# Setup of a two-layer attention and feed-forward kernel: where the first steps' moves, loads and mask work are issued

## The reference

```
x = x + cross_attention_0(layernorm(x), ctx, mask, Wq, bq, Wk, bk, Wv, bv, Wo, bo)   # 16 heads of 16, 77 context tokens
x = x + experts(layernorm(x))             # 6 experts of width 128, top 2 by a router
x = x + cross_attention_1(layernorm(x), ctx, w_q, w_kv, w_concat)                    # 16 query heads, one shared key/value head
x = x + fixed_point_mlp(layernorm(x))     # 256 -> 1024 -> 256, piecewise linear gelu, rounding to 1/256
# attention: softmax(q k^T / 4 + mask) v, for 77 keys a batch
```

## Time and profile before

| what | value |
|---|---|
| median of 3 runs | 789.33 us (789.02 to 789.87) |
| the profiled execution's own time | 787.69 us |
| its span | 785.5 us |
| TensorE busy | 729.2 us, 93% |
| VectorE, ScalarE, GpSimd busy | 644.6, 514.0, 373.0 us |

### The profile page before, as it was taken

The page is one execution under the profiler, slowest core; times in us unless marked ns, Lnnn a source line. Parts: engine busy times, 40 slices in busy tenths (PEclk is TensorE's granted clock), DMA queues, the critical chain, the costliest instruction groups (busy, mean ns, idle before and its releaser), DMA issues.

```text
span 785.5 us, 13554 instructions
## 1 busy us (share of the span) xinstructions
PE 729.2 (93%) x4372; PEld 549.3 (70%) x4372; DVE 644.6 (82%) x1546; ACT 514.0 (65%) x943; POOL 373.0 (47%) x323
## 2 busy tenths in 40 slices
PE   4799999999999999999997999999989999999995
PEld 3566666766558888888874555555568888888985
DVE  7648778777878878888897888998788999999995
ACT  3446556565654456555436777677778989989885
POOL 6374444334222223232214232232259999999884
PEclk9889999999999999999999999999999999999999
DMA  7975634654210000001029665755200000000001
GB/s 234 134 209 121 139 76 93 119 120 88 68 36 1 1 1 7 1 1 55 1 41 143 89 82 76 131 76 77 30 1 1 2 28 28 28 28 2 28 28 54
DMA packets 25101, 48.64 MB, mean 62 GB/s; under 512 B 3686, under 2 KB 7016, under 8 KB 24520
## 3 DMA queue, kind: packets, MB, share of 16 engines
q1 hardware_dynamic: 23366, 46.54, 30.6%
q10 hardware_dynamic: 1666, 1.24, 0.5%
HBM read 12.12 MB, written 4.19 MB: 21 GB/s over the span
## 4 chain that ended last, share of the span: by engine, by line
PE 54%; DVE 19%; issue 8%; ACT 7%; DMA 7%; POOL 4%; SPq 0%; ACTq 0%; DVEq 0%; POOLq 0%
PE bank L141 15%; PE bank L649 6%; PE bank L436 6%; PE bank L413 6%; DMA qst<-mt 5%; PE bank L424 5%; PE bank L388 5%; DVE mx L342 4%; PE bank L416 3%; DVE fpart L768 3%; PE bank L812 3%; PE bank L391 2%; DVE x L617 2%; DVE fyl L780 2%; DVE ffixed L762 2%
## 5 line engine op out<-in xcount | busy, mean ns | idle before, releaser
L316 ACT ACTIVATE pt<-bank 77x512 f32<-77x512 f32 x256 | 141.1, 589 | 78.2 <-PE bank L416 58.3
L342 DVE TENSOR_REDUCE mx<-bank 128x4 f32<-128x308 f32 x256 | 109.0, 471 | 22.5 <-PE bank L391 12.3
L413 PE MATMUL bank<-qst,l_kst 128*77 128x512 f32 (+1 forms) x256 | 102.8, 417 | 15.8 <-DMA qst<-mt 9.8
L721 POOL TENSOR_TENSOR frise<-fg,fg 128x512 f32<-128x512 f32 x64 | 101.3, 1583 | 6.7 <-ACT fg L739 1.5
L388 PE MATMUL bank<-l_kblk,qh 128*128 128x308 f32 x256 | 81.3, 336 | 10.1 <-DVE mx L342 5.7
L284 POOL TENSOR_TENSOR ol<-ot,oh 128x512 fp32r<-128x512 f32 x32 | 41.4, 1294 | 94.4 <-ACT oh L321 50.2
L617 DVE SCALAR_TENSOR_TENSOR x<-bank,eweight,x 128x256 f32<-128x256 f32 x192 | 79.6, 477 | 4.1 <-PE bank L649 3.8
L413 PEld LDWEIGHTS bank<-qst,l_kst 128*77 128x77 f32 (+1 forms) x256 | 36.5, 146 | 65.1 <-ACT pt L316 24.1
L103 POOL TENSOR_TENSOR rstd<-var,minus_half 128x4 f32<-128x4 f32 x32 | 34.4, 1076 | 100.1 <-DVE var L98 52.2
L114 ACT ACTIVATE xn<-x,shift,rstd 128x256 f32<-128x256 f32 (+1 forms) x128 | 67.2, 594 | 17.1 <-POOL shift L105 17.1
L388 PEld LDWEIGHTS bank<-l_kblk,qh 128*128 128x128 f32 x256 | 48.0, 192 | 42.8 <-issue 33.1
(11 more groups left out here) (176 smaller groups left out, 2117.0 us busy)
## 6 DMA issues: line engine op xcount, KB each, us to landing
qst<-qh SPq DMA_DIRECT2D x64, 256.0 KB, 6.5
qst<-ql SPq DMA_DIRECT2D x32, 256.0 KB, 8.8
out<-x SPq DMA_DIRECT2D x8, 512.0 KB, 2.6
qst<-ml SPq DMA_DIRECT2D x8, 480.0 KB
x<-in_x SPq DMA_DIRECT2D x3, 1024.0 KB, 12.4
weights<-in_mlp_w SPq DMA_DIRECT2D x2, 1024.0 KB, 5.0
mraw<-in_mask SPq DMA_DIRECT2D x8, 154.0 KB
x<-in_x SPq DMA_DIRECT2D x2, 512.0 KB, 5.8
```

Source lines behind the costliest of these rows:

```text
L316: self.nc.scalar.activation(self.pt[0:T, i // 4 % 2, i % 4, :], self.bank_of(G, i)[0:T, :], ACT.Exp).then_inc(self.probs, 1)
L342: self.nc.vector.reduce_max(out, banks[u % len(banks)][:, 0:4 * T].rearrange("q (p par t) -> q p par t", p=2, par=2), AX.X).then_inc(self. ...
L413: last = self.nc.tensor.matmul(out, layer.kst[rows, layer.stack(c * HC + 2 * k + par), b * T:(b + 1) * T], self.qst[rows, self.slot(G), c ...
L721: self.nc.gpsimd.tensor_tensor(self.rise[:, k % 2, :], self.g1[:, k % self.R, :], self.g0[:, k % self.R, :], ALU.subtract).then_inc(self.r ...
```

## The change

Seven edits, all in the setup and in steps 0 to 2. (1) The move of block 0's maxima is issued by ScalarE instead of SyncE. (2) The values of batch 0 are computed between the turn of block 0 and its query projection; batches 1 to 3 stay behind the maxima, and ScalarE takes the first two batches' values before the norm of block 1. (3) The two loads of the last 2 MB of `x` leave the setup; each stands in step 0 and step 1 of SyncE's program, behind that step's query moves and ahead of the next mask's load and of `stack_maxima`, with a semaphore of its own. (4) The load of mask 1 is issued between the two halves of step 0's moves. (5) GpSimd builds the key blocks of batches 1 to 3 as soon as VectorE has written those of batch 0, ahead of the inversion for block 1. (6) GpSimd splits mask 1 before step 0's loop and not in it. (7) In step 0 the projection of block 1's queries stands behind scores 1 and 2 instead of 0 and 1, ScalarE's `leading` behind exponentials 2 and 4 instead of 0 and 1, VectorE's second `rest` behind maxima 0 and 1, and units 2 and 3 stand at i = 6 instead of 4.

```diff
--- before.py
+++ after.py
@@ -873,7 +873,7 @@
         fw1 = raw(0, F)
         fw2 = weights[:].rearrange("p (c d) -> p c d", d=D)
 
-        x0_in, x1_in, x2_in, xr_in = sem("x0_in"), sem("x1_in"), sem("x2_in"), sem("xr_in")
+        x0_in, x1_in, x2_in, xr_in = sem("x0_in"), sem("x1_in"), sem("x2_in"), [sem(f"xr_in{k}") for k in range(2)]
         k_in, q_in, c_in, vo_in = sem("k_in"), sem("q_in"), sem("c_in"), sem("vo_in")
         cleared = sem("cleared")
         kst_clear, kst_const = sem("kst_clear"), sem("kst_const")
@@ -911,21 +911,18 @@
                         for k, part in enumerate((l0.kh, l0.kl, l0.kh)):
                             sp.dma_start(l0.kst[32 * k + 16 * par:32 * k + 16 * par + 16, c * HC + par:(c + 1) * HC:2, :].bitcast(F32),
                                          part[64 * par:64 * par + 64, c, :].bitcast(F32)).then_inc(kst_in[c], 16)
+                    att.stack_queries(sp, 0, c)
                     if c == 0:
-                        att.stack_queries(sp, 0, 0)
-                att.stack_maxima(sp, 0)
-                att.stack_queries(sp, 0, 1)
-                att.load_mask(sp, 1, d["mask"])
-                for b in range(2, B):
-                    tiles = slice(2 * b * NT, 2 * (b + 1) * NT)
-                    sp.dma_start(x[:, tiles, :], d["x"][:, tiles, :]).then_inc(xr_in, 16)
-
+                        att.load_mask(sp, 1, d["mask"])
                 for G in range(BLOCKS):
                     n = G + 1
                     if n < BLOCKS:
                         att.stack_low(sp, n)
                         for c in range(C):
                             att.stack_queries(sp, n, c)
+                        if G < 2:
+                            tiles = slice(2 * (G + 2) * NT, 2 * (G + 3) * NT)
+                            sp.dma_start(x[:, tiles, :], d["x"][:, tiles, :]).then_inc(xr_in[G], 16)
                         if n + 1 < BLOCKS:
                             att.load_mask(sp, n + 1, d["mask"])
                         att.stack_maxima(sp, n)
@@ -997,20 +994,21 @@
                 att.mask_parts(pool, 0)
                 nc.gpsimd.memset(att.pt[64:P, :, :, :], 0.0).then_inc(pt_clear, 1)
                 pool.wait_ge(pt_clear, 1)
-                norm.invert(pool, 1)
-                pool.wait_ge(kt_ready, 1)
+                pool.wait_ge(kblk_ready, 1)
                 for head in range(H):
                     c, h = divmod(head, HC)
                     nc.gpsimd.tensor_tensor(l0.kblk[:, c, 1:B, h, :],
                                             l0.kh[:, c, T:BT].bitcast(F32).rearrange("p (b t) -> p b t", b=B - 1),
                                             hsel[:, h:h + 1].unsqueeze(2).to_broadcast([P, B - 1, T]), ALU.mult).then_inc(kblk_more, 1)
                     pool.wait_ge(kblk_more, head + 1)
+                norm.invert(pool, 1)
+                att.mask_parts(pool, 1)
                 pool.wait_ge(woh_ready, 1)
                 nc.gpsimd.tensor_tensor(l0.wol[:], wo0, l0.woh[:].bitcast(F32), ALU.subtract).then_inc(wol_ready, 1)
                 pool.wait_ge(wol_ready, 1)
 
                 for G in range(BLOCKS):
-                    if G + 1 < BLOCKS:
+                    if 0 < G < BLOCKS - 1:
                         att.mask_parts(pool, G + 1)
                     norm.invert(pool, G + 2)
                     if G > 0:
@@ -1135,9 +1133,11 @@
                                          klowf[96:P, par, :].unsqueeze(1).unsqueeze(1).to_broadcast([32, HC, B, T]),
                                          ACT.Copy).then_inc(kst_const, 1)
                 att.maxima(act, 0, FIRST_MAX[0])
-                norm.norm(act, 1)
-                act.wait_ge(v_clear, 2)
+                att.stack_maxima(act, 0)
                 for k in range(2):
+                    if k == 1:
+                        norm.norm(act, 1)
+                    act.wait_ge(v_clear, 2)
                     act.wait_ge(v_done, k + 1)
                     nc.scalar.activation(l0.vall[0:T, 2 * k:2 * k + 2, :, 0:DH],
                                          att.SC[k][0:T, :].rearrange("t (b h d) -> t b h d", b=2, d=DH), ACT.Copy).then_inc(v_ready, 1)
@@ -1151,7 +1151,9 @@
                     p, n, nm = G - 1, G + 1, G + 2
                     for h in range(H):
                         att.exp(act, G, h)
-                        if h < C and n < BLOCKS:
+                        if G == 0 and h in (2, 4):
+                            att.leading(act, 1, h // 4)
+                        if G > 0 and h < C and n < BLOCKS:
                             att.leading(act, n, h)
                         if h == 2 and p >= 0:
                             if p == 0:
@@ -1312,15 +1314,18 @@
                     p, n, nm = G - 1, G + 1, G + 2
                     if G < 2:
                         dve.wait_ge(x2_in, 16)
-                    if G == 2:
-                        dve.wait_ge(xr_in, 16 * 2)
+                    if G in (2, 4):
+                        dve.wait_ge(xr_in[G // 4], 16)
                     if nm >= BLOCKS:
                         dve.wait_ge(att.added, 2 * (nm - BLOCKS + 1))
                     norm.moments(dve, nm)
                     if n < BLOCKS:
-                        for c in range(C):
-                            att.rest(dve, n, c)
+                        att.rest(dve, n, 0)
+                        if G > 0:
+                            att.rest(dve, n, 1)
                         att.take_maxima(dve, n, range(0, 2), att.X)
+                        if G == 0:
+                            att.rest(dve, n, 1)
                     if p >= 0:
                         att.unfold(dve, p, 3)
                     if n < BLOCKS:
@@ -1509,6 +1514,17 @@
                 pe.wait_ge(q_in, 32)
                 for c in range(C):
                     norm.turn(pe, 0, c, att.W[c])
+                def values(b):
+                    bank = att.SC[b // 2][0:T, D * (b % 2):D * (b % 2) + D]
+                    for k in range(C):
+                        nc.tensor.matmul(bank, ctx[:, k, b * T:(b + 1) * T], wv0[:, k, :], start=(k == 0), stop=False)
+                    last = nc.tensor.matmul(bank, ones_row[:, :], rows[:], start=False, stop=True)
+                    if b % 2:
+                        last.then_inc(v_done, 1)
+
+                pe.wait_ge(vo_in, 64)
+                pe.wait_ge(cleared, 1)
+                values(0)
                 pe.wait_ge(wql_ready, 1)
                 for c in range(C):
                     att.queries(pe, l0, 0, c)
@@ -1517,15 +1533,8 @@
                 for u in range(16):
                     att.max_unit(pe, l0, 0, u, FIRST_MAX)
                 att.turn_maxima(pe, 0, FIRST_MAX[0])
-                pe.wait_ge(vo_in, 64)
-                pe.wait_ge(cleared, 1)
-                for b in range(B):
-                    bank = att.SC[b // 2][0:T, D * (b % 2):D * (b % 2) + D]
-                    for k in range(C):
-                        nc.tensor.matmul(bank, ctx[:, k, b * T:(b + 1) * T], wv0[:, k, :], start=(k == 0), stop=False)
-                    last = nc.tensor.matmul(bank, ones_row[:, :], rows[:], start=False, stop=True)
-                    if b % 2:
-                        last.then_inc(v_done, 1)
+                for b in range(1, B):
+                    values(b)
                 for c in range(C):
                     pe.wait_ge(att.ql_ready, c + 1)
                     norm.turn(pe, 1, c, att.W[c])
@@ -1539,18 +1548,20 @@
                         if G == 0 and i == HC:
                             pe.wait_ge(kst_in[1], 16 * 6)
                         att.score(pe, l0, G, i)
-                        if i < C and n < BLOCKS:
+                        if G == 0 and i in (1, 2):
+                            att.queries(pe, l0, 1, i - 1)
+                        if G > 0 and i < C and n < BLOCKS:
                             att.queries(pe, l0, n, i)
                         if i == 1 and p >= 0:
                             att.weigh(pe, l0, p, 3)
                         if i == 2 and G == 1:
                             pe.wait_ge(kblk_more, H)
-                        if i in (2, 4, 7, 9) and n < BLOCKS:
+                        if i in (2, 4, 7, 9) and n < BLOCKS and (G > 0 or i != 4):
                             for u in {2: (0, 1), 4: (2, 3), 7: (8, 9), 9: (10, 11)}[i]:
                                 att.max_unit(pe, l0, n, u, att.X)
                         if i == 6:
                             if n < BLOCKS:
-                                for u in (4, 5):
+                                for u in (2, 3, 4, 5) if G == 0 else (4, 5):
                                     att.max_unit(pe, l0, n, u, att.X)
                             att.weigh(pe, l0, G, 0)
                             if n < BLOCKS:
```

## The result

The changed kernel takes 792.23 us in the median of six runs (791.6 to 793.89) against 789.17 us (787.84 to 789.9): a ratio of 1.0041, 95% interval 1.0028 to 1.0055. It is slower by 0.4%. The forecast was 788.0 us with a range of 783.5 to 790.1, and 792.23 lies outside it. The profiled execution took 792.07 us with a span of 789.8 us, 4.3 us longer than before.

The account below looks back on a forecast made before the run. TensorE, 93% busy, bounds the kernel, so removed idle counts. Step 0 gains 5.8 us, 2.7 returns waiting for block 1's maxima, 1.8 to the clock: net 1.3, 789.33 to 788.0 us, range 783.5 to 790.1.

Parts of the forecast that it names:

- landed at 34 to 35, hidden by the turn: Setup: block 0's maxima move on ScalarE's queue takes 4 to 5 us, so the first score starts at 35.6.
- Rival E: Setup: the move on ScalarE's queue waits all the same, first score near 40.5; gain 1.2 us, 788.1; chance 10%.
- rival D: Step 1: slower, as the lagging engine keeps its loaded pace and block 1's maxima land after 62.6; example 790.9; chance 12%.
- Key blocks, inversion, norm, values: Setup: GpSimd's key blocks 10.34 us, inversion ends 32.45, norm 34.55, TensorE's values near 34.0, turn 35.6.
- Plus 0.4 for mask 1: Lagging engine's work before block 1's maxima: the mask load moved ahead adds 0.4 us to 43.3.
- Step 0: Step 0: clock stays up, small losses from reordering; score 7 starts at 46.7 instead of 52.50, 5.8 us sooner.
- 0.5 plus 0.8 forecast: Step 0 losses: block 1's projection waits for `xl`, about 0.5 us; later `leading` bunches units 2 to 5, about 0.8.
- The 2.1 us of clock: Step 0: without the idle hole before the first score the clock stays up, gaining 2.1 us.
- Rival B: Step 1: the clock holds despite the wait; gain 3.1 us, 786.2; chance 13%.
- The lagging engine: DMA: one engine carries the 94 KB mask move and lags; block 1's maxima wait for it, step 1 starts at 61.3.
- The term of 15.1 us for step 1's set: Lagging engine: step 1's mask and query moves take it 15.1 us, as from 48.7 to 63.8 before, reaching 58.8.
- the sum: Lagging engine's work from 43.3: 0.4, 15.1, 2.5 for `x`, 0.6 for maxima, less 0.6, giving step 1 at 61.3.

Follow-up runs that it names:

- only the mask moved away: Changed kernel with the load of mask 1 moved to 16 us, behind step 0's mask moves, maxima's move still on ScalarE's queue: 791.81 us, ratio 1.0031.
- the split: Kernel before with the 94 KB mask move of 47 partitions split into 32 and 15 in every step: 791.73 us, ratio 1.0036.
- Where the first score was early: Changed kernel with block 0's maxima move on SyncE's queue ahead of the second half's keys: 791.32 us, ratio 1.0033.
- the queries first: Changed kernel, edits 1 and 7 undone, mask 1 at 16 us, both halves' query moves before maxima, `x` behind next maxima, 94 KB split: ratio 1.0001.

## Why the prediction was wrong

**The step that failed** is "landed at 34 to 35, hidden by the turn": the price of the maxima's move on ScalarE's queue. It landed near 43, some 13.6 us after its issue at 29.55. I took 4 to 5 us between 2.94 (empty) and 10.6 (behind the backlog) where the far end was right, and not even far enough: leaving SyncE's program also let the query moves go ahead of it. The edit alone costs 0.36%. I had weighed two sections of the page "DMA: Bandwidth & Descriptors" of the Trainium skill here. With that of "Issuing engines are not separate DMA queues" (only the issue time is saved) the runs agree: the move landed no sooner by its own queue. The alternation of "Queues, rings and completion order" shows in no packet for 9 us. Rival E stood on the first and named the mechanism, but with the old landing of 40.5 and a free queue afterwards it priced a gain of 1.2 us; rival D had the sign from another place.

This step was not the only one that sufficed. The mask, priced at 0.4 us (below), delays the first score as much by itself. With only edit 1 undone it starts at 42.78, with only the mask moved away at 43.67, with edits 1 and 4 undone at 41.01.

**Key blocks, inversion, norm, values** were right: GpSimd's sixteen operations took 10.35 us from 20.90 on, beside VectorE's reductions, the norm ended at 34.8 (34.55 forecast), the turn at 36.0 (35.6).

**"Plus 0.4 for mask 1"** was wrong: the run with edit 4 alone has 2.6 us in this place, when it stands ahead of the maxima.

**Step 0.** Edit 7 was priced rightly: it costs 1.3 us (0.5 plus 0.8 forecast). The 2.1 us of clock could not be gained, as the hole grew: six matmuls take 2.48 us at 45.12. Missed was the wait of the second `leading` for block 0's second `ql` move; with the first score at 36.2 it held step 0, and the clock fell there (0.50 in 48 to 50) after all. Rival B's remark that gaps of 0.4 to 1 us leave the clock up failed here: gaps of 1.01 and 0.43 us came before that fall.

**The lagging engine** was right as a mechanism (the split takes the whole wait of the first score away) and has a part in the changed kernel's first score, whose last packets came when most engines were done. It did not decide step 1 there: block 1's maxima were issued at 64.72, and their move took 3.02 us. Where the first score was early, it did: step 1 at 65.8, not 61.3. The term of 15.1 us for step 1's set was mis-sized: from the landing of `ql` (44.3) to step 1's first score that run took 21.5 us, where the sum had 18.0 (43.3 to 61.3). With the mask's moves already done, the query moves run alone, at 125 GB/s:

```profile
57.00:58.00 1.00, 1.00 (x7) 0.82 (x6) 0.78 (x3) 0.37 (x1) 0.00 (x0) 1.00 1.06 125
```

against 193 in the kernel before at nearly the same share. There the mask's moves were issued just ahead of them. So having mask 1 early (edits 4 and 6), which I took for free here, goes with a lower rate of the query moves behind it: the run with edit 1 undone has 128 to 130 GB/s between 54 and 60 us, that with edit 4 undone as well 191 to 236. What sets the rate was not found.

**Left open.** Why 154 KB cost 2.6 us between the halves; whether packets of one queue's moves are carried strictly in order of issue (the first packets on ScalarE's queue fit, the landing at 39.6 with the queries first is 2.6 us later than I had worked out by it); what sets the rate of the query moves; and how the 3.4 us at step 1 divide between the edits, since those measured alone do not add.

## What to carry to other kernels

When the DMA engines are saturated, move an urgent transfer ahead in the order of issue (first score at 36.2), not to another engine's queue (43.2); and when a wait leaves a queue's program, ask what it held back that now goes ahead. Before a start is moved forward, follow the buffers of the next block too: the wait that is second in line, and the clock that falls behind it, set what the first is worth. The version with mask 1 loaded in the idle time at 16 us, the maxima ahead of the keys and `x` behind the next maxima is faster than the kernel before by 0.13% and, with the 94 KB split, by 0.18%; the two are not told apart.

## What the runs showed of the hardware

With a DMA share of 1.0 to 1.1, block 1's query moves (each writes 32 partitions) ran at 117 to 131 GB/s between 52 and 61 us in the changed kernel, where the mask's moves had been issued 9 us ahead. In the kernel before, where these were issued just ahead, it was 180 to 215 between 54 and 60 us, and with the 94 KB move split 137 to 152. A move of 32 KB on ScalarE's queue had its first packet some 9 us after its issue while SyncE's queue was loaded, and in the run of edit 1 alone it was carried by 42 us, while 2 MB that SyncE had issued 1 us later were under way until 47. The 94 KB move of 47 partitions left one engine behind: a share of 0.06 at 25 GB/s in 62 to 64 us of the run with the maxima ahead of the keys; split into 32 and 15 partitions, the first score's wait of 4.09 us was gone.
